# Merged softmax denominators through an accumulating DMA, and a reordered SP queue, in a gated cross-attention layer

## The reference

```python
x = x + jnp.tanh(g_xattn[0]) * xattn(_layernorm(x), ctx, mask, mask, Wq, bq, Wk, bk, Wv, bv)
x = x + jnp.tanh(g_ffn[0]) * ffn(_layernorm(x), W2, scale, scale1)

# xattn, per batch and head:
q = Wq @ target + bq;  k = Wk @ source + bk;  v = Wv @ source + bv
dot = q^T k / sqrt(32);  dot = mask * dot - (1 - mask) * 1e6
amap = softmax(dot, axis=-1) * mask;  out = amap @ v
# ffn: both operands rounded to float8_e4m3, then a matrix product over the last axis
```

## Time and profile before

| | us |
|---|---|
| median of 3 runs | 2500.13 (2499.8 to 2501.52) |
| profiled execution | 2498.55 |
| its span in the trace | 2496.9 |
| PE busy | 2441.7 (98%) |
| DVE / POOL / ACT busy | 1960.7 / 1643.2 / 1387.1 |

### The profile page before, as it was taken

How to read it: one execution, slowest core, us unless ns; L and a number is a source line. 1 busy time by engine, 2 the same in 40 slices (tenths; PEclk the granted TensorE clock), 3 DMA queues, 4 the chain that set the end, 5 groups by cost and what they waited for, 6 DMA issues and landing times.

```text
span 2496.9 us, 40504 instructions
## 1 busy us (share of the span) xinstructions
PE 2441.7 (98%) x13116; PEld 1382.0 (55%) x13177; DVE 1960.7 (79%) x3259; ACT 1387.1 (56%) x2606; POOL 1643.2 (66%) x1259
## 2 busy tenths in 40 slices
PE   7999999999999999999999999999999999999997
PEld 5888888875444444444444444444444444444442
DVE  6677776687788888888888888888888888888885
ACT  3333333315666666666666666666666666666664
POOL 2443333426777777777777777777777777777775
PEclk9999999999999999999999999999999999999999
DMA  6766666664444444444444444444444444444411
GB/s 245 262 243 237 234 235 235 227 188 100 94 102 98 102 101 102 97 94 95 94 93 100 92 92 92 92 92 101 92 93 95 99 101 102 98 101 97 104 45 56
DMA packets 241807, 313.48 MB, mean 126 GB/s; under 512 B 75000, under 2 KB 142648, under 8 KB 241624
## 3 DMA queue, kind: packets, MB, share of 16 engines
q1 hardware_dynamic: 230776, 275.56, 44.0%
q10 hardware_dynamic: 10848, 35.66, 4.0%
HBM read 199.83 MB, written 101.38 MB: 121 GB/s over the span
## 4 chain that ended last, share of the span: by engine, by line
PE 94%; DVE 1%; DMA 1%; issue 1%; POOL 1%; ACT 1%; SPq 0%; POOLq 0%; ACTq 0%; DVEq 0%
PE bank L863 22%; PE bank L893 20%; PE bank L848 20%; PE bank L878 19%; PE bank L904 9%; PE bank L940 4%; PE bank L933 1%; POOL pair_sum L398 1%; DMA q_st<-qx_scr 0%; DMA w_nat<-in_L_xattn_Wk_dram 0%; DMA v_scr<-stage 0%; ACT probs L715 0%; DVE x_raw L1043 0%; PE bank L802 0%; PE bank L924 0%
## 5 line engine op out<-in xcount | busy, mean ns | idle before, releaser
L398 POOL TENSOR_TENSOR pair_sum<-probs 128x512 f32<-128x512 f32 x1020 | 1279.2, 1286 | 399.0 <-ACT probs L715 399.0
L1143 DVE TENSOR_REDUCE part_max<-bank 128x1 f32<-128x512 f32 x2048 | 1276.6, 682 | 242.7 <-PE bank L878 229.2
L715 ACT ACTIVATE probs<-bank 128x512 f32<-128x512 f32 x2048 | 1067.4, 604 | 601.7 <-PE bank L863 578.7
L863 PE MATMUL bank<-q_st,k_st 100*128 100x512 f32 x2048 | 866.3, 425 | 6.0 <-ACT probs L715 6.0
L878 PE MATMUL bank<-k_st,q_st 98*128 98x512 f32 x2048 | 817.4, 399 | 8.3 <-DVE part_max L1143 6.5
L863 PEld LDWEIGHTS bank<-q_st,k_st 100*128 100x128 f32 x2048 | 387.4, 190 | 410.3 <-issue 211.2
L893 PE MATMUL bank<-probs,v_t 128*32 128x512 f32 x4096 | 545.6, 605 | 0.0
L878 PEld LDWEIGHTS bank<-k_st,q_st 98*128 98x128 f32 x2048 | 388.7, 190 | 129.2 <-DVE part_max L1143 15.8
L389 POOL TENSOR_TENSOR stage_lo<-stage,stage_hi 128x512 fp32r<-128x512 f32 x128 | 186.6, 1483 | 137.7 <-ACT stage_hi L661 136.2
L904 PE MATMUL bank<-pair_sum,ones 128*32 128x512 f32 x2040 | 265.5, 592 | 0.0
L661 ACT ACTIVATE stage_hi<-stage 128x512 fp32r<-128x512 f32 x128 | 80.2, 633 | 205.1 <-DVE stage L1007 142.9
(11 more groups left out here) (112 smaller groups left out, 2007.3 us busy)
## 6 DMA issues: line engine op xcount, KB each, us to landing
k_st<-k_scr SPq DMA_DIRECT2D x96, 512.0 KB
q_st<-q_scr SPq DMA_DIRECT2D x192, 256.0 KB
c_raw<-in_ctx_dram ACTq DMA_DIRECT2D x32, 512.0 KB, 7.0
k_scr<-stage_hi SPq DMA_DIRECT2D x64, 256.0 KB, 2.5
k_scr<-stage_lo SPq DMA_DIRECT2D x64, 256.0 KB, 2.7
v_scr<-stage SPq DMA_DIRECT2D x64, 256.0 KB, 2.9
q_scr<-stage_hi SPq DMA_DIRECT2D x64, 256.0 KB, 2.4
q_scr<-stage_lo SPq DMA_DIRECT2D x64, 256.0 KB, 2.7
```

Of the source, the lines that this page charges most:

```text
L398: nc.gpsimd.tensor_tensor(pair_sum[:, r % 2, h], probs[:, a, h], probs[:, a + 1, h], ALU.add).then_inc(pair_done, 1)
L715: nc.scalar.activation(probs[:, c % PR, h, :], s_bank_of(n, k)[:, :], ACT.Exp).then_inc(exp_done, 1)
L863: nc.tensor.matmul(s_bank_of(n, k)[:, :], k_st[p][0:KS, h, j * P:(j + 1) * P], q_st[p][0:KS, th, h, :], start=True, stop=True).then_inc(sc ...
L1143: nc.vector.tensor_reduce(part_max[:, th, sh, at:at + 1], x_bank_of(n, "tile", k)[:, :], AX, ALU.max).then_inc(max_done, 2)
```

## The change

**Four sum buffers and a merge.** The two buffers of `pair_sum` and the idle `stage` and `stage_hi` become a ring `sums` of four; pair sum r goes to buffer r % 4. After r = 1 and r = 5, POOL issues one DMA that adds buffer 0 onto buffer 1 (`merge`, 128 x 2048 fp32, 8 KB per partition, accumulating). PE has six groups per quad in place of eight: r = 2, merged (0+1), r = 3 after slots 27, 35, 43, and 6, merged (4+5), 7 after slots 59, 3, 11. The group of the merged sum waits for the DMA. Before the first quad's first add POOL waits until the stores of `stage` and `stage_hi` have landed.

**SP.** `stack_q` is split by half. At the period's start only k is loaded. The queries of half 1 of quad n+1 go behind `move_den` and `load_res` (slot 12 and after), those of half 0 of quad n+2 behind `load_v` (slot 32 and after). `set_max` goes ahead of `move_inv`, the transpose behind `spread_inv`.

**The rest.** The feed-forward groups go from slots 31 and 47 to 39 and 51. DVE's split of the maxima uses two small reductions at 19 and 51, one small ACT operation at 20 and 52 (`minus_high`) and one small reduction on DVE at 22 and 54 (`low_max`); PE multiplies by a negated identity. DVE's `invert` is only the reciprocal, at 19 and 51; gate times mask is made by ACT once per quad (slot 46), and POOL multiplies by it after r = 2 and r = 6 (`mask_inverse`). `weigh` is split by half: half 0 after r = 2, half 1 after r = 3. Steps 13 and 14 of the rounding go from slot 19 to 27.

```diff
-            F_JOBS = {23: "max1", 31: "ffn0", 47: "ffn1", 55: "max0"}
+            F_JOBS = {23: "max1", 39: "ffn0", 51: "ffn1", 55: "max0"}
+            DEN_AT = {27: 0, 35: 1, 43: 2, 59: 3}
+            DEN_AFTER = {3: 4, 11: 5}
+            NG = 6
+            SUM_OF_GROUP = (2, 1, 3, 6, 5, 7)
+            GROUP_OF_SUM = {1: 1, 2: 0, 3: 2, 5: 4, 6: 3, 7: 5}
+            MERGED = (0, 4)
...
+            sums = [pair_sum[:, 0], pair_sum[:, 1], stage[:, :, :], stage_hi[:, :, :].bitcast(F32)]
...
+                    def merge(n, th):
+                        pool.wait_ge(pair_done, QH * (SJ * n + 4 * th + 2))
+                        pool.dma_start(sums[1], sums[0], accum_op=ALU.add).then_inc(merged[th], 16)
+
+                    def mask_inverse(m, th):
+                        pool.wait_ge(inv_done, 2 * (2 * m + th) + 1)
+                        pool.wait_ge(gates_masked, m + 1)
+                        nc.gpsimd.tensor_tensor(inv_c[:, :], inv_c[:, :], gtm_c[:, th], ALU.mult).then_inc(inv_done, 1)
...
                     def period(n, p):
                         for r in range(SJ):
+                            if n == 0 and r == 0:
+                                wait_stage_free()
                             if real(n) and (n, r) != (LAST, SJ - 1):
                                 add_pair(n, r)
+                            if real(n) and r % 4 == 1:
+                                merge(n, r // 4)
+                            if r == 2 and ordinary(n - 1):
+                                mask_inverse(n - 1, 1)
+                                weigh(n - 1, 0)
+                            if r == 6 and real(n):
+                                mask_inverse(n, 0)
                             if r == 3 and ordinary(n - 1):
-                                weigh(n - 1)
+                                weigh(n - 1, 1)
                                 add_residual(n - 1, 1 - p)
...
                     def period(n, p):
                         if n > 0 and real(n + 1):
                             stack_k(n + 1, 1 - p)
-                            stack_q(n + 1, 1 - p)
                         if ordinary(n - 1):
                             move_den(n - 1, 1)
                             load_res(n - 1, 1 - p)
-                        if ordinary(n - 2):
-                            turn_y8(n - 2)
-                        if ordinary(n - 1):
-                            move_inv(n - 1, 1)
+                        if n > 0 and real(n + 1):
+                            stack_q(n + 1, 1, 1 - p)
                         if real(n):
                             set_max(n, 1, p)
                         if ordinary(n - 1):
+                            move_inv(n - 1, 1)
                             spread_inv(n - 1, 1)
+                        if ordinary(n - 2):
+                            turn_y8(n - 2)
                         if real(n):
                             load_tm(n)
                         if real(n + 1):
                             load_v(n + 1, 1 - p)
+                        if real(n) and real(n + 2):
+                            stack_q(n + 2, 0, p)
                         if real(n):
                             move_den(n, 0)
                         if ordinary(n - 2):
                             store(n - 2, p)
-                        if real(n):
-                            move_inv(n, 0)
                         if real(n + 1):
                             set_max(n + 1, 0, 1 - p)
                         if real(n):
+                            move_inv(n, 0)
                             spread_inv(n, 0)
                         if n == LAST:
                             load_res(n, p)
...
-                        pe.wait_ge(pair_done, QH * SJ * m + QH * (r + 1))
+                        if i == 1:
+                            pe.wait_ge(merged[th], 16 * (m + 1))
+                        else:
+                            pe.wait_ge(pair_done, QH * SJ * m + QH * (r + 1))
...
-            FFN_AT = (31, 47)
+            FFN_AT = (39, 51)
...
-                    NORM_AT_2 = {3: (11,), 11: (12,), 19: (13, 14)}
+                    NORM_AT_2 = {3: (11,), 11: (12,), 27: (13, 14)}
```

More of the change, by code:

```diff
@@ L187, in flamingo_gated_layer @@
         pair_done = sem("pair_done")
+        merged = [sem(f"merged{i}") for i in range(TH)]
         pv_done = sem("pv_done")
@@ L295, in run_batches @@
                 batch(B - 1, False)
[L297 removed]
+            STACK_DMAS = 4
             NORM_STEPS = 15
```

220 lines of the change are left out of this document (138 added, 82 removed).

## The result

The changed kernel takes 2531.78 us, median of 4 runs (2528.18 to 2534.52), beside 2500.40 for the kernel before on the same chip: ratio 1.0124, 95% interval 1.0107 to 1.0142. I had forecast 2452 (2438 to 2490). It is 1.2% slower where 1.9% faster was forecast. The profiled execution has a span of 2526.4 us in place of 2496.9.

What follows compares the result with a forecast made beforehand. PE's own instruction list was taken to bound the kernel (98% busy, 94% of the chain). 2498.55 - 55.7 + 3 + 1 + 7 - 2 = 2451.9, forecast 2452 us, range 2438 to 2490.

Steps and rivals of the forecast that it cites:

- The merge: Accumulating DMA after r = 1 and 5: lands in 9 us, PE asks 13.0 us after POOL's adds, cost 0.
- rival B: Merge takes longer than 13 us, PE waits at slots 35 and 3: time 2548 to about 2760; chance 0.14.
- SP's queue: Order of DMA issues on SP: `set_max`, denominators' transfer and transpose land in time, cost 0; a stall gone gains 2 us.
- The remaining groups: PE's six groups left per quad: no term for when r = 2 and r = 6 are now asked for.
- Start: POOL's first add waits about 5 us for the last stores, taken up by its room: 1 us.
- End: Last quad's inversion waits for POOL's last adds, which delays the last residual's load: +5 to +9 us, 7 taken.
- The turn: PE's turn at slot 23, just after `low_max`: loses 0 to 0.3 us, 64 times; 0.05 taken, 3 us.
- 64 groups x 0.87: Two denominator groups fewer per quad over 32 quads, each worth 0.87 us on PE: 55.7 us saved.
- the gapless timeline: PE's rows follow each other without a gap, so a removed group is worth its full 0.87 us.
- The 0.52 us for a group: A denominator group's cost on PE as read from 265.5 us over 255 groups, rejected in favour of 0.87 us.
- The second row: DVE starts the maxima of slots 20 to 23 at 1238.15, 2.48 us for four, leaving 0.2 us before PE's turn.
- rival C: Removed groups are not on the path, or waits eat exactly the gain: 2495 to 2505; chance 0.03.

Runs made afterwards that it cites:

- e10: Changed kernel with the spread cut in four and a later wait for the first stores, merges and their waits left out: 2477.45 us, beside 2494.10 with merges.
- e3: Changed kernel with the spread of the inverted denominators cut in four transfers of 32 partitions: 2494.5 us, ratio 0.9975 to the kernel before.
- e5: Changed kernel with the spread left whole and k's load issued ahead of it on SP's queue: 2501.00 us, ratio 1.0006 to the kernel before.
- e11: e10 with the groups after slots 27 and 59 taking r = 1 (5), those after 35 and 3 r = 2 (6): 2449.57 us.
- e8: Changed kernel with cut spread and later wait for the first stores; groups of r = 2, 3, 6, 7 wait head by head: 2481.95 us, base 2494.10.
- e2: Changed kernel with the groups of r = 2 and 6 asked for after slots 31 and 63, not 27 and 59: 2529.86 us, ratio 1.0112.
- e9: Kernel before, without PE's groups after slots 19 and 51 and nothing in their place: 2494.72 us, beside 2503.60 for the kernel before.

## Why the prediction was wrong, step by step

- **The merge (right in its time, short in its cost).** I took 9 us, it measured 8.5; its issue on POOL 0.88 us (0.5 to 2 given; 1.06 at most in this kernel, so no merge started 2.4 us late). PE never waits for the merged sum, and rival B did not come. The cost of 0 was too low: by e10 the merges cost 6 us in thirty periods, and 9 us at the start. As the Trainium skill's DMA: Bandwidth & Descriptors (Anatomy of one DMA) would have it, 1 MB would be 4.4 us, or 6.8 with the second operand counted, both estimates; the trace has 8.5 us and disagrees with both. I spent most of the argument on the one step that was unseen, and the time was lost on steps that were in plain sight.
- **SP's queue (wrong, 35 us).** This part priced `set_max`, the transpose and `move_den`, and nothing of k, 1.6 MB asked for at slot 19. It did not follow the second `move_inv`, now behind `set_max` and POOL, to the spread that hangs on it and to k behind that. "I take 0, since the engines serve several queues" was the assumption, and the stretch with a share of 0.27 speaks for a transfer that did not use all of them. That k is late behind the spread is shown by e3 and e5. The waits that the part did price were near: `set_max` costs some 2 us at slot 32, the late transpose 2 us, and the two stalls of the kind in the earlier trace rows (0.72 and 0.73 us) are gone, for which I had allowed 2 us.
- **The remaining groups (wrong, 22 us in the windows).** The part on the merge worked out when PE asks for the merged sum and never when it asks for r = 2 and r = 6, which the table in the diff moves a group ahead. From the earlier trace rows and the timeline it could be worked out: POOL begins its adds about 1.5 us after the scores of slot 20 and needs 5.02 us, 6.5 in all, and PE asks 6.3 us after these scores. Shown by e11; e8 and e2, read alone, would have led to DVE.
- **Start (wrong, 15 us in place of 1).** "About 5 us, taken up by POOL's room": the room is 1.96 us per eight slots, the wait was 19.05. I counted the stores and not what SP had issued ahead of them.
- **End (right, but for the last link).** +7 forecast (5 to 9), 8.3 measured (82.0 to 90.3). The chain ran as I gave it down to the spread; then DVE waits 8.33 us for the spread itself and 0.47 for the residual's load, which I had taken as the one that ends last.
- **The turn (0 in place of 3 us).** The windows with a turn are no longer by `low_max`: window 20 takes 3.23 where k is in time (3.24 before), and what window 52 has more stands ahead of the turn and comes from the feed-forward group that moved to slot 51.
- **64 groups x 0.87 (right in this kernel, for a wrong reason).** e11's period is 57.80 us, 1.88 under before. But the reason, "the gapless timeline" of PE, does not show it: e9 has the same timeline to start from and yields 9 us. PE's row says nothing of how close behind it DVE runs. (The 0.52 us for a group in the same part is a slip: 265.5 us over 255 groups are 1.04 us each; 0.87, from the starts of rows, does not hang on it.) The second row, DVE's maxima at 1238.15, has no bracket for idle time; that row spoke for rival C, to which I gave 0.03.

By the ledger, with a group at 0.87 us: up to quad 1 the forecast was 1 - 1.7 and 14.5 were measured, 15 us more; in thirty periods -52 + 3 - 2 = -51 and 6.7, 58 us more, of which 35 are k and 22 r = 2 and 6; from quad 31 on 7 - 1.7 and 8.3, 3 us more. Together they are the 76 us between 2451.9 and the profiled execution (2528.18). So the miss has three steps: k's wait behind the spread, taken as nothing; POOL's newest sum asked for a group earlier, not looked at; and the wait at the start, priced at 1 us.

## What to carry to other kernels

When a step is taken out of a table, list for every step that remains when its input is ready and when it is now asked for; the ones that the change seems not to touch move too. On a queue that issues in order, price each entry that stands behind something new, by its bytes and by its user, and ask of each transfer over how many engines it spreads. And before a removed step is counted in full, take it out alone, or look whether the next engine has a gap in the same window: what it covered may be all of its worth.
